# Moving two small operations of an edge attention from VectorE to ScalarE: the rescaling of the running sums, and the placing of the weights

## What is computed

```
Q, K, V = (enh @ Wq + bq), (enh @ Wk + bk), (enh @ Wv + bv)      # N x 4 x 64
mod_k   = K[src] + 0.2 * rel_w[edge_relations][:, None, :]
scores  = einsum('ehd,ehd->eh', Q[dst], mod_k) / 8
ex      = exp(scores - segment_max(scores, dst)[dst])
agg     = segment_sum(ex / segment_sum(ex, dst)[dst] * V[src], dst)
out     = layernorm(agg @ Wo + bo + node_features)
```

## Time and profile before

| | us |
|---|---|
| median of 3 runs | 6748.72 (6743.35 to 6772.54) |
| the profiled execution | 6708.42 |
| its span, first to last instruction | 6706.8 |
| stage l3e, first gather to last merge | 4883.8 to 6567.9 |

### The profile page before, as it was taken

One profiled execution on the slowest core, in us unless ns is written; L12 is line 12 of the kernel. 1 busy time (PEld: TensorE's weight loads), 2 busy tenths in 40 slices (PEclk: granted clock), 3 DMA queues, 4 the chain that ended last, 5 costly groups with the idle time before them and its releaser, 6 DMA issues. The chain is left out here.

```text
span 6706.8 us, 90264 instructions
## 1 busy us (share of the span) xinstructions
PE 4342.6 (65%) x24913; PEld 3150.9 (47%) x24913; DVE 3458.5 (52%) x6689; ACT 2184.9 (33%) x7656; POOL 3192.9 (48%) x3187
## 2 busy tenths in 40 slices
PE   6996676766677744544444546887646666666676
PEld 4664454544445423333333435766335555555553
DVE  4452666666666662211111231112558888888885
ACT  1221455555545430000000111222225454555541
POOL 0422566666666236676676520002145565655551
PEclk8896777777777876666766778998778888888885
DMA  4334666666666525333333407882366666666673
GB/s 133 126 123 163 182 197 199 202 196 198 198 196 197 125 72 186 93 93 93 92 95 92 72 29 243 261 262 87 108 189 205 203 210 203 205 207 203 201 185 102
DMA packets 509932, 1077.03 MB, mean 161 GB/s; under 512 B 94770, under 2 KB 322388, under 8 KB 505993
## 3 DMA queue, kind: packets, MB, share of 16 engines
q0 software_dynamic: 204144, 617.42, 32.6%
q1 hardware_dynamic: 296854, 452.03, 20.2%
q10 hardware_dynamic: 8512, 2.74, 0.2%
HBM read 964.49 MB, written 194.54 MB: 173 GB/s over the span
## 5 line engine op out<-in xcount | busy, mean ns | idle before, releaser
L772 POOL DMA_INDIRECT l0e_kv<-t_table,k_recs x912 | 986.1, 1081 | 636.9 <-ACT l0e_vw L1049 375.5
L772 POOL DMA_INDIRECT l3e_kv<-t_table,k_recs x912 | 971.0, 1065 | 667.5 <-ACT l3e_vw L1049 368.0
L1464 PE MATMUL l2e_pA<-l2e_row,l2e_oh 128*128 128x257 f32 x1824 | 633.4, 516 | 768.7 <-issue 380.4
L1418 POOL DMA_INDIRECT l2e_row<-t_table,l2e_idx x912 | 899.7, 986 | 389.7 <-issue 265.4
L1464 PEld LDWEIGHTS l2e_pA<-l2e_row,l2e_oh 128*128 128x128 f32 x1824 | 460.0, 262 | 942.0 <-issue 852.9
L1006 PE MATMUL l0e_pA<-l0e_vw,l0e_ohf 128*128 128x260 f32 x1824 | 643.9, 500 | 198.3 <-ACT l0e_vw L1049 129.2
L958 PE MATMUL l3e_pQE<-l3e_qb,l3e_ohT 128*128 128x256 bf16 x2736 | 428.0, 318 | 405.9 <-issue 378.7
L1049 ACT ACTIVATE l3e_vw<-l3e_kv,l3e_w 128x64 f32<-128x64 f32 x2736 | 679.8, 334 | 0.0
L1049 ACT ACTIVATE l0e_vw<-l0e_kv,l0e_w 128x64 f32<-128x64 f32 x2736 | 679.6, 334 | 0.0
L1443 DVE SCALAR_TENSOR_TENSOR l2e_acc<-l2e_acc,k_itf,l2e_pA 128x257 f32<-128x257 f32 x228 | 109.9, 482 | 1058.6 <-issue 981.9
L1006 PEld LDWEIGHTS l0e_pA<-l0e_vw,l0e_ohf 128*128 128x128 f32 x1824 | 427.7, 247 | 338.5 <-ACT l0e_vw L1049 156.6
(11 more groups left out here) (469 smaller groups left out, 7126.8 us busy)
## 6 DMA issues: line engine op xcount, KB each, us to landing
exp_w<-in_L_gnn_w SPq DMA_DIRECT2D x224, 512.0 KB
t_table<-l0n_tab SPq DMA_DIRECT2D x26, 2048.0 KB, 6.9
l0e_qb<-t_q SPq DMA_DIRECT2D x228, 192.0 KB
l3e_qb<-t_q SPq DMA_DIRECT2D x228, 192.0 KB
t_agg<-l0e_acc SPq DMA_DIRECT2D x228, 130.0 KB
t_agg<-l3e_acc SPq DMA_DIRECT2D x228, 130.0 KB
l0e_drow<-t_drow SPq DMA_DIRECT2D x57, 512.0 KB
l3e_drow<-t_drow SPq DMA_DIRECT2D x57, 512.0 KB
```

Source lines behind the costliest of these rows:

```text
L772: pool.indirect_dma_start(kv[:, n % SK, g, :], None, table[:, :], bass.IndirectOffsetOnAxis(ap=K["recs"][:, n, g, ridx:ridx + 1], axis=0)) ...
L1418: pool.indirect_dma_start(row[:, s, g, 0:D], None, table[:, :], bass.IndirectOffsetOnAxis(ap=idx[:, i, g:g + 1], axis=0)).then_inc(row_rea ...
L1464: last = pe.matmul(pA[s % 2][:, 0:W], oh[:, s, g, :], row[:, s, g, :], start=(g == 0), stop=(g == G - 1))
```

## The change

Only stage l3e changes; for l0e (`first`) the program is the same. DVE no longer copies the weights to place 65 of `vw`, and no longer rescales. ACT does both: one 128x16 copy ahead of its first value scaling of an item, and a rescaling in four instructions of 128x65, one for each head, since ACT takes one scale for each partition and instruction. `merge` stays on DVE and waits for `part_done`, which ACT now raises. ACT's `rescale(t-3)` stands at the head of its iteration t and waits for `item_done`, which DVE's merge of the item before raises. ACT's loop runs two iterations longer.

```diff
@@ weigh (DVE)
-                dve.tensor_copy(vw[:, v, :, :, DK], w[:, m % 2, j, :, :])
+                if first:
+                    dve.tensor_copy(vw[:, v, :, :, DK], w[:, m % 2, j, :, :])
@@ loop (DVE)
-                if 0 <= r < NI:
+                if first and 0 <= r < NI:
                     rescale(r)
@@ weigh (ACT)
+                if not first and g0 == 0:
+                    act.activation(vw[:, v, :, :, DK], w[:, m % 2, j, :, :], ACT.Copy)
@@ loop (ACT)
-            for t in range(0, NI + 1):
+            def rescale(n):
+                m, j = n // BI, n % BI
+                act.wait_ge(fac_ready, m + 1)
+                if n:
+                    act.wait_ge(item_done, n)
+                for h in range(H):
+                    last = act.activation(part[:, h, :], acc[:, (n - 1) % BI, h, :], ACT.Copy, scale=fac[:, m % 2, h, j:j + 1])
+                last.then_inc(part_done, 1)
+
+            for t in range(0, NI + (1 if first else 3)):
                 m, j = divmod(t, BI)
-                y = t - 1
+                y, r = t - 1, t - 3
+                if not first and 0 <= r < NI:
+                    rescale(r)
                 if live(m) and j == 1:
                     weights(m)
-                if y >= 0:
+                if 0 <= y < NI:
                     widen(y)
                     weigh(y, 0, 1)
                 if live(m) and j == 0:
                     turned_ends(m)
-                if y >= 0:
+                if 0 <= y < NI:
                     weigh(y, 1, AW)
```

## The result

The changed kernel takes 6824.8 us (median of 4 runs, 6820.0 to 6829.8) against 6746.0 us before (4 runs, 6739.6 to 6772.5): **79 us more, ratio 1.0107, 95% interval 1.0083 to 1.0132**. (The ratio of the two medians alone would be 1.0117.) The forecast was 6757.5 us with a range to 6788. The change is slower, clear of the noise though by less than 2%, and by more than the range allowed. Of the forms written down, rival (b) comes nearest in time, but it turns out to be only part of the loss.

The account below looks back on a forecast made before the run. It took each block to be bound by a chain of transfers, PE and ACT, with DVE itself only for 5.25 of 27.67 us; -2.9 + 0.5 + 7.2 + 4.0 = +8.8 on 6748.7 gave 6757.5 us, range 6728 to 6788.

Parts of the forecast that it names:

- rival (b): Merge of j = 2: part late in every block; 6772 us at upper ends, 6804 in strong form; chance 8% for the latter.
- a block's chain and its three parts: Block of 27.67 us: 8.78 transfers and PE, 13.64 with PE and ACT, 5.25 DVE itself; removed instructions outside the last.
- the price of the moved instructions: Per item in l3e: DVE saves 0.41 us (93 over 228 items); ACT pays 0.96 for rescaling and 0.12 for copy.
- rival (a): DVE bounds the stage: 93 us go, less 4 at the end, 6660 us; half-way form 6722; chance for both 9%.
- when part is ready: Rescaling of j = 2 on ACT: part done at 5652.2, 5.2 us behind the start of z.
- the stage's end: After the last keys ACT sets the pace: 3.4 us ahead of the last scalings plus 0.6 behind, 4.0 us paid.
- the slack at the merge of j = 2: Part ready 0.36 us before the merge; about 42 of 56 full blocks safe, 14 shorter, costing 6 x 0.7 + 7 x 0.35.
- I take it for PE: Wait of 1.03 us ahead of keys of j = 2, releaser "remote": ascribed to PE, expected to grow by 0.75.
- strong form: Merge of j = 2: a rescaling at DVE-like 0.42 a head makes part late, 46 us more, 6804 us; chance 8%.
- Gain: nothing: In plain blocks DVE's saved time becomes longer waits before keys and candidates; only 7 store-wait blocks gain, 2.9 us.
- Rival (c): Shifted gathers meet SP's query load in the block's first part: 0.3 us per block, 17 us, 6775 or 6740; chance 10%.

Follow-up runs that it names:

- e4: Kernel before, l3e without copy and rescaling on any engine (DVE relieved, nobody gets the work), first kind of chip: 6750.2 us against 6708.5, ratio 1.0067.
- h3: Kernel before, l3e without copy and rescaling on any engine, repeated on another chip of the first kind: 6744.1 us against 6706.6, ratio 1.0059.
- i3: Kernel before, l3e without copy and rescaling on any engine, repeated on a third chip of the first kind: 6789.3 us against 6750.8, ratio 1.0055.
- g1: The changed kernel again, on a chip of the second kind, against the kernel before (6049.2 us): 6107.3 us, ratio 1.0099.
- f1: Kernel before plus one spare, unread copy per item on ACT, second kind of chip: 6069.0 us against 6067.2, ratio 1.0006.
- h1: Changed kernel with only the rescaling due at j = 2 one iteration earlier on ACT, first kind of chip: 6755.3 us against 6706.6 before, ratio 1.0064.
- i2: Changed kernel with only the rescaling due at j = 2 one iteration earlier on ACT, another first-kind chip: 6826.9 us against 6750.8 before, ratio 1.0105.
- e3: Kernel before plus four spare 128x65 activations per item on ACT, DVE keeping its work, first kind of chip: 6708.9 us against 6708.5, ratio 1.0001.
- g2: Kernel before with the row loads last on SP in the last edge attention, second kind of chip: 5933.5 us against 6049.2, ratio 0.9804.
- g4: Changed kernel, row loads last on SP, rescaling of j = 2 one iteration earlier on ACT, second kind: 5874.6 us against 6049.2 before, ratio 0.9706.
- i1: Changed kernel, row loads last on SP, rescaling of j = 2 one iteration earlier on ACT, first kind: 6824.9 us against 6750.8 before, ratio 1.0100.

## Why the prediction was wrong

**Right.** The places of a block's chain and its three parts; the price of the moved instructions (DVE -90, ACT +245 us); that DVE's relief brings no gain in this order (rival (a) fell: e4, h3, i3); when part is ready (5.15 us after z against 5.2); the stage's end (3.7 against 4.0).

Two steps failed. On the kind of chip of the result the second one made the number: of the 2.23 us per block, 2.20 lie ahead of z, in parts that the forecast put at nothing (or at 0.5 us in all). The first shows undisturbed on the second kind.

**Wrong, first: the slack at the merge of j = 2.** The step reads: "The merge started at 5652.56. Slack 0.36 us", with 42 of 56 blocks safe. That slack was measured from merges that stood behind a wait, the 1.03 us ahead of the keys of j = 2. I had costed this wait as one that stays, even grows by 0.75. It vanished in most blocks: keys 2.31 us after z on the mean instead of 2.93, and 1.68 in g1. The forecast took this wait for PE's work ("I take it for PE"). PE it was, but not its work: L965 had ended at 5648.47, and its signal is recorded at 5650.07, 1.6 us later, 0.1 us before keys. In f1, where the signals come at once, keys follow z by 2.10 us in the kernel before, with no wait at this place. Without it the merge could come 2.40 us behind those keys, at z + 4.1, and part comes at z + 5.15. Term: 7.2 us forecast for 14 blocks; measured a wait of 0.8 us in 37 of some 50 blocks here, 30 us in all, and 1.03 us in every block of g1. (Here the earlier keys gave back nearly all of it, the 0.03 us of the table.) That is rival (b), by another road than I had written: not a dearer rescaling, but a nearer merge. On the second kind of chip it is most of the +58 us by the table, 0.71 of 0.91 us per block; there "(b) in nearly every block" was the outcome, and I had given its strong form 8%.

**Wrong, second: "Gain: nothing", taken to mean cost nothing.** The relief was costed by what DVE's time is worth, never by what an earlier DVE sets off, and the waits on PE were taken for fixed work. Rival (c) had the right object and the wrong size and cause, 0.3 us per block by shifted gathers. Measured: 37 to 42 us for the relief alone (e4, h3, i3), about 0.7 us per block; in the whole change the second query load 3.3 us later against the row load, and PE's signals 1.5 us per block later. On the second kind the first part of the table grew by 0.30 us, the size that (c) had; that shifted gathers are the cause isn't shown.

How the 79 us divide on the first kind isn't settled. The relief alone costs about half by e4. The rest should be the hand-over, but with the lateness mended the loss was 1.0064 in h1 and 1.0105 in i2, with intervals that hardly meet, on two chips; and in the traces the two aren't additive, since z to the end of L807 grew by 0.03 us only. The stage of the profiled i2 is 56 us longer than that of h1, and 29 of these are PE's busy time (1174 and 1145 us for the same matmuls), so the clock has a share in that difference. The forecast's reading of the earlier trace rows was off in a smaller way too: the four rows hold 135 waits in 54 blocks, 2.5 per block of 1.4 us, not a little over three of one.

**Open.** What delays PE's signals and SP's instructions on chips of the first kind. Seen: SP's 0.7 us gaps, and PE's semaphore updates up to 6 us after the matmul, while those of DVE and ACT, where they are recorded, mostly follow within 0.02 us. Also seen: of the semaphore updates by the compute engines in l3e, 2420 of 3306 are recorded in the trace of before, 2509 in the changed kernel's, and 3300 and 3306 in f1 and g1. In before, updates are missing above all in l0e, l2e and l3e, the three stages with 912 gathers each (75%, 50% and 73% recorded), and PE's signals are late on the mean in the same three; in l0n and l3n, 98 and 100% are recorded and PE's follow within 0.02 us. Every time here comes with a recorded span, so whether the recording itself holds these chips back can't be told; no run is without it. Not seen as a cause: the packets, whose durations agree (4096 bytes on the gathers' queue: median 159 ns on both, mean 228 and 224), the gathers on POOL (1.25 us apart when back to back, on both), ACT's load (e3). A version in which DVE is held back without work, or reads through other ports, wasn't tried.

The Trainium skill, Perfetto Trace Analysis, section Identifying the Most-Contended Engine, calls the engine with the highest occupancy the most contended one, to be optimized first; the forecast's rival (a) read that as taking work off it. Read so, it failed where that engine waited three times in a block (e4, h3, i3), and held from g2 to g4, where it had waited for 0.6 us in 1200: there 59 us came out of 93 that were taken off. DVE was the busiest engine both times (81% of the stage before, 97% in g2). That it is the busiest doesn't tell the two apart; its waits do.

## What to carry to other kernels

When work is moved to another engine, compute when the result is ready, and compare it with the earliest time at which the reader could come once *its* waits are gone too, not with the time it came before. Taking work off an engine that waits in every block wasn't free here on the first kind of chip: test the relief without the hand-over (work left out, nobody gets it), and look for a transfer order that makes the engine the bound first. When the profile names no believable releaser for a wait, compare the end of the last producer with the time of its semaphore's update: that tells a slow producer from a late signal. Run the parts of a change on more than one chip; here the same change loses 1% on both kinds, in different parts of the block, and the order that mends one kind makes the other slower.

## What the runs showed of the hardware

- The kernel before takes 6707 to 6751 us on three chips and 6049 to 6067 on two, 11% apart, with the same transfers. It isn't spread evenly: the first edge attention takes 1658 and 1304 us, l3e 1680 and 1528 (before and f1), while l0n, ahead of them, takes 595 to 607 in every run.
- On the first kind PE's semaphore updates come late in l3e: that of the ends turned 0.96 us after the matmul on the mean before, 1.65 in the changed kernel, against 0.01 in f1 and g1.
- On the first kind SP's instructions stand 0.69 to 0.724 us apart in stretches of l3e (98 such gaps in the whole program before, 369 in the changed kernel, 430 in i1; 12 to 19 in the runs on the second kind).
- Twelve products of 128x256 took PE 2.72 us after 6.62 us of idleness, at 1.2 GHz, and 1.47 us later in the same block, at 2.4.
- An activation of 128x65 with a scale per partition costs ACT 0.24 us by starts (1.05 for four in a group, end to end), like one of 128x64; a copy of 128x16 0.11.
